# Cross attention's products with V issued in two halves, in a new order beside the scores; all heads written out; small changes at routing and at the expert tiles

## The reference, cut to what matters

```python
# cross attention, per head: 2048 queries, 1601 keys, 16 values each
scores = jnp.einsum('bhqd,bhkd->bhqk', q, k) / jnp.sqrt(jnp.float32(D_HEAD))
attn = jax.nn.softmax(scores, axis=-1)
out = jnp.einsum('bhqk,bhkd->bhqd', attn, v)
...
# experts
router_logits = jnp.einsum('bth,eh->bte', x, router_w)
topk_values, topk_indices = jax.lax.top_k(router_logits, TOP_K)
h1 = jax.nn.gelu(jnp.einsum('bth,efh->btef', x, w1) + b1, approximate=False)
expert_outputs = jnp.einsum('btef,ehf->bteh', h1, w2) + b2
```

## Time and profile before

| what | us |
|---|---|
| median of 3 runs (lowest to highest) | 2126.51 (2116.33 to 2149.73) |
| profiled execution, its own time | 2127.89 |
| span of the profile | 2126.1 |

### The profile page before, as it was taken

One profiled execution on the slowest core, in us unless ns is written; L12 is line 12 of the kernel. 1 busy time (PEld: TensorE's weight loads), 2 busy tenths in 40 slices (PEclk: granted clock), 3 DMA queues, 4 the chain that ended last, 5 costly groups with the idle time before them and its releaser, 6 DMA issues.

```text
span 2126.1 us, 35541 instructions
## 1 busy us (share of the span) xinstructions
PE 1815.0 (85%) x10422; PEld 930.1 (44%) x10422; DVE 1372.8 (65%) x2296; ACT 1190.3 (56%) x2400; POOL 360.3 (17%) x575
## 2 busy tenths in 40 slices
PE   6908899999899999987588888888888984999994
PEld 2504334333333333325243333333333244899993
DVE  6506899899898999815578888888888034011113
ACT  1200577777777777774047777777777541333333
POOL 6104022222222222110000000000000003233331
PEclk9956799999999999999579999999999565999997
DMA  6420001100001000002101001000002113566664
GB/s 232 164 101 16 3 25 36 35 28 25 27 26 34 28 35 27 3 1 78 61 32 65 26 21 38 21 27 32 20 31 68 40 42 119 151 204 192 192 193 136
DMA packets 72612, 140.12 MB, mean 66 GB/s; under 512 B 14140, under 2 KB 47309, under 8 KB 70237
## 3 DMA queue, kind: packets, MB, share of 16 engines
q1 hardware_dynamic: 64746, 127.84, 18.1%
q0 software_dynamic: 7712, 10.37, 2.3%
HBM read 109.07 MB, written 28.45 MB: 65 GB/s over the span
## 4 chain that ended last, share of the span: by engine, by line
PE 64%; DVE 17%; issue 6%; DMA 5%; ACT 4%; SPq 3%; POOL 1%; DVEq 0%; POOLq 0%; ACTq 0%
PE banks L910 19%; PE banks L900 16%; PE banks L862 12%; DVE CM L1317 6%; PE banks L1083 5%; PE banks L1093 5%; DMA W<-in_w1T_dram 2%; ACT XT L1149 2%; DVE wset L1324 2%; PE banks L816 2%; DVE skip L1324 2%; DVE CM L1320 2%; PE banks L820 1%; ACT late L1149 1%; PE banks L873 1%
## 5 line engine op out<-in xcount | busy, mean ns | idle before, releaser
L1149 ACT ACTIVATE XT<-banks 128x512 f32<-128x512 f32 x1240 | 671.9, 599 | 354.9 <-PE banks L900 249.6
L862 PE MATMUL banks<-oper 52*128 52x512 f32 (+1 forms) x2048 | 716.8, 446 | 107.5 <-DVE CM L1317 70.2
L900 PE MATMUL banks<-oper 54*128 54x512 f32 x1856 | 702.4, 465 | 37.4 <-ACT XT L1149 17.2
L1317 DVE TENSOR_REDUCE CM<-banks 128x1 f32<-128x804 f32 x512 | 486.4, 991 | 104.5 <-PE banks L862 104.5
L900 PEld LDWEIGHTS banks<-oper 54*128 54x128 f32 x1856 | 320.6, 191 | 428.1 <-ACT XT L1149 241.2
L862 PEld LDWEIGHTS banks<-oper 52*128 52x128 f32 x2048 | 344.1, 197 | 333.8 <-DVE CM L1317 202.9
L1149 ACT ACTIVATE late<-banks 128x512 f32<-128x512 f32 x616 | 337.5, 599 | 117.3 <-PE banks L900 101.3
L910 PE MATMUL banks<-XT,VS 128*32 128x512 f32 x2480 | 346.9, 632 | 2.7 <-ACT XT L1149 1.4
L1224 ACT ACTIVATE HID<-banks,b1E 128x128 f32<-128x128 f32 x312 | 89.1, 369 | 182.8 <-PE banks L1083 182.2
L1490 DVE TENSOR_TENSOR YB<-banks,b2E 128x256 f32<-128x256 f32 x39 | 16.6, 425 | 258.7 <-PE banks L1093 258.7
L910 PE MATMUL banks<-late,VS 128*32 128x512 f32 x1232 | 169.3, 622 | 0.8
(11 more groups left out here) (210 smaller groups left out, 1452.4 us busy)
## 6 DMA issues: line engine op xcount, KB each, us to landing
W<-in_w1T_dram SPq DMA_DIRECT2D x39, 1024.0 KB, 5.5
oper<-kD SPq DMA_DIRECT2D x32, 256.0 KB
W2R<-in_w2T_dram SPq DMA_DIRECT2D x8, 1024.0 KB, 8.5
oper<-kxD SPq DMA_DIRECT2D x32, 208.0 KB
b2E<-in_b_dram SPq DMA_DIRECT2D x39, 128.0 KB
qD<-parts SPq DMA_DIRECT2D x8, 512.0 KB, 2.7
kD<-parts SPq DMA_DIRECT2D x8, 512.0 KB, 2.7
oper<-kD SPq DMA_DIRECT2D x32, 128.0 KB
```

Source lines behind the costliest of these rows:

```text
L862: mm = pe.matmul(slot[:, n * QB:n * QB + ch], QO[64 * g:64 * g + M_ROWS, c2, col:col + P], KO[64 * g:64 * g + M_ROWS, c2, k0:k0 + ch], sta ...
L900: pe.matmul(bank, KO[64 * g:64 * g + S_ROWS, c, b * P:(b + 1) * P], QO[64 * g:64 * g + S_ROWS, c, q0:q0 + QB], start=True, stop=True).then ...
L1149: act.activation(PT[(c * plan.nu + u) % PRING], S[(c * plan.nu + u) % SBANKS], ACT.Exp).then_inc(A.exps, 1)
L1317: dve.tensor_reduce(CM[:, a, b:b + 1], slot.rearrange("p (n k) -> p n k", n=2)[:, :, 0:ch], AX.XY, ALU.max).then_inc(A.freed, 1)
```

## The change

- The head loop is gone: `head_steps` issues all 16 heads written out, on all engines, in both attentions.
- In cross attention each batch of V products is issued in two parts, queries 0 to 255 of each block and then 256 to 511 (`vparts` 2). The order within a slot is now a string of tokens: S0 to S3 the scores, m half a fill, V0 and V1 the parts of V. It is one string for slots with two fills and one for those with three. `order` gives the scores other query blocks so that neighbours fall into different groups. Self attention keeps its order.
- Norms: ACT saves the turned stream of group g-1 before it waits for the scales of group g, and PE does the router of group 2 before it turns group 3.
- Routing: DVE makes both halves of `OL`, POOL makes half of `OV` (the part with the tile numbers) in two instructions.
- Experts: SP issues the first weights of tile i ahead of the biases of tile i-2. The rows of tile i+2 are turned and saved where those of tile i+1 were, and ACT runs one small gelu before the first tile.
- `single` (one bank to a ring slot) is False in both plans and has no effect.

```diff
-    def __init__(self, nk, chunk, causal):
+    def __init__(self, nk, chunk, causal, single, vparts, sequences):
...
-        return (2, 0, 1, 3) if self.first((b + LEAD) % self.nb) % 2 == 0 else (0, 2, 3, 1)
+        if self.first((b + LEAD) % self.nb + 1) - self.first((b + LEAD) % self.nb) == 2:
+            kinds = (1, 1, 0, 0)
+        else:
+            kinds = (1, 0, 0, 1)
+        lead = self.first((b + LEAD) % self.nb) % 2
+        free = [[0, 1], [2, 3]]
+        return tuple(free[(kind + lead) % 2].pop(0) for kind in kinds)
...
-SELF = Plan(TT, QB, True)
-CROSS = Plan(NXP // P, XCH, False)
+SELF = Plan(TT, QB, True, False, 1, {2: "m S0 m S1 m S2 m V0 m S3"})
+CROSS = Plan(NXP // P, XCH, False, False, 2, {2: "S0 m S1 m V0 S2 m m S3 V1", 3: "m S0 m S1 m m S2 V0 m S3 m V1"})
...
-            body(0, 0, 0)
-            with engine.Fori(0, HEADS_LOOPED // RING) as it:
-                for c in range(RING):
-                    h = it * RING + (1 + c)
-                    body(h, (1 + c) % RING, it + (1 + c) // RING)
-            for h in range(HEADS_LOOPED + 1, H):
+            for h in range(H):
                 body(h, h % RING, h // RING)
...
-            for i in range(NTILES):
-                load_tile(i)
+            experts = []
+            for i in range(NTILES + WBUF - 1):
+                if i < NTILES:
+                    experts.append(expert_of(i))
+                    load_weights(i, experts[i])
+                if i >= WBUF - 1:
+                    load_biases(i - (WBUF - 1), experts[i - (WBUF - 1)])
...
-            pool.wait_ge(s_seat, 1)
-            for t in range(TT):
-                ins = pool.tensor_scalar(OL[:, TT + t, :], seatLo[:, :], lo[:, 1, t:t + 1], None, ALU.is_equal)
-            ins.then_inc(s_lot, 1)
+            pool.wait_ge(s_oh, 1)
+            for c in range(2):
+                half = slice(c * TT, (c + 1) * TT)
+                pool.tensor_tensor(OV[:, half, 1, :], OH[:, half, :], turns[:, :].unsqueeze(2).to_broadcast([P, TT, NBLK]),
+                                   ALU.mult).then_inc(s_lot, 1)
...
+                    w = QB // plan.vparts
+                    cols = slice(part * w, (part + 1) * w)
                     for n in range(4):
                         qb = plan.order(b)[n]
-                        mm = pe.matmul(OA[32 * qb:32 * qb + 32, :], VS[:, c, b, :], PT[(c * plan.nu + 4 * b + n) % PRING],
+                        mm = pe.matmul(OA[32 * qb:32 * qb + 32, cols], VS[:, c, b, :], PT[(c * plan.nu + 4 * b + n) % PRING][:, cols],
                                        start=(b == 0), stop=(b + 1 == nk), skip_group_check=True)
-                    mm.then_inc(A.pv, 1)
+                    if part + 1 == plan.vparts:
+                        mm.then_inc(A.pv, 1)
...
-                for g in range(NG - 2, NG):
-                    turn_stream(g)
-                    if call:
-                        router(g - 1)
+                turn_stream(NG - 2)
+                if call:
+                    router(NG - 3)
+                    router(NG - 2)
+                turn_stream(NG - 1)
...
             transpose_tile(0)
+            transpose_tile(1)
             for i in range(NTILES):
                 first_layer(i)
-                if i + 1 < NTILES:
-                    transpose_tile(i + 1)
+                if i + 2 < NTILES:
+                    transpose_tile(i + 2)
...
+            act.activation(odds[:, 3, :], odds[:, 0, :], ACT.Gelu)
             save_rows(0)
+            save_rows(1)
```

115 lines of the change are left out of this document (62 added, 53 removed).

## The result

| kernel | median us (lowest to highest, executions) | ratio to before, 95% interval |
|---|---|---|
| before | 2126.51 (2115.58 to 2149.73, 5) | 1 |
| changed | 2077.5 (2063.8 to 2131.93, 5) | 0.9724 (0.966 to 0.9788) |
| changed, six more executions | 2079.32 (2033.97 to 2109.41) | |

The change is a gain of 2 to 3%, about half of what was forecast (2010 us, range 1985 to 2066). One thing is needed to read the numbers: executions of the changed kernel differ by up to 98 us, by how long TensorE's clock stays at half, and the ratio is made from the quicker ones. The eleven lie almost on a line, from 2033.97 us at a mean granted clock of 0.922 to 2131.93 at 0.868. In time at half clock (twice the missing part of the clock, times the span) that is 317 against 562 us: each further microsecond at half clock costs 0.40. The median execution of the five has 432 us of it.

A forecast was written before the change was run, and what follows sets the result against it. No engine was saturated in cross attention, so a chain between PE, DVE and ACT was the bound. Self attention -19, cross attention -51, tail and transposes -34, norms -2, routing -5, experts -7: -118 from 2127.9, 2010 us, range 1985 to 2066.

The forecast's parts named there:

- heads 1 to 13, most of head 0 and half of head 14, 14.3 heads: Cross attention: heads counted as gaining 3.55 us each (35.4 for 38.95) from the split, -51 us; bounds -72 and -14.
- the clock falls in the tail again: Rival, end of cross attention: half clock returns because a 0.9 us gap remains; 2047 us in all, chance 0.20.
- bridge 0.77 us, and neither bridges 1.21: Cross attention: with PE away 0.77 us per half batch instead of 1.21, ACT and DVE keep working; 35.4 us a head.
- the two-part price 0.12 + 0.88: Cross attention's V batch: 0.12 us fixed plus a clock-scaled part; half a batch 0.12 + 0.44 = 0.56 at full clock.
- the 19 forecast: Self attention: writing out the head loop removes branch stalls, half-clock slots behind them and register work; -19 us, bounds 0 and 19.
- The waits come back: Rival, cross attention: waits reappear elsewhere in PE's fixed order, losing half the gain per head; 2035 or 2070 us, chance 0.15.
- fetched too slowly: Rival: the longer straight code cannot be fetched fast enough, so self attention's gain is lost; 2029 us, chance 0.06.
- nothing in cross attention: Rival: DVE sets the pace in cross attention anyway, so the change gains nothing there; 2061 us, chance 0.05.
- a half takes as long as a whole: Rival, cross attention: records, not columns, hold a half batch, costing 0.44 us more per half; 2193 us, chance 0.04.
- the forecast 2: Norms and router: half the last router run moves ahead of the last transposes, ACT saves earlier; -2 us, bounds -3.3 and 0.
- 4.1 of 5: Routing: DVE starts OL earlier since two products go to POOL, ending at 1788 for 1793.20; -5 us, bounds -6 and -2.
- the forecast 7: Experts: -2 us from rows saved before the table load and gelus, -5 from first weights issued a whole tile earlier.

## Why the prediction was wrong

**The step that failed** is the count of "heads 1 to 13, most of head 0 and half of head 14, 14.3 heads" at 3.55 us each. It took over from the kernel before that the clock is back at 1089, and priced every head at full clock. At half clock a head takes 60.5 us, 24.8 more. The first profile spent heads 0 to 2 and a part of head 3 so, the next one a part of head 0. The prediction had a rival for the clock, but only for the tail, and none of its five put it at the start. What the runs showed in its place: with V in halves the clock comes back 39 to 348 us behind the first score of head 0 (14.4 once), where it had been 11.7 in the kernel before. That the halves do this in the first heads is shown; by what means is open.

**What it cost.** The two columns are 112.5 us over the forecast in the first profile. The start holds 75.6 of it: 21.6 on the way to the first save, 2 x 24.8 for the next two heads and 4.4 for the third (40.11 for 35.73). In the tail the clock fell as well: the last two heads took 97.3 us, against 67.1 in the second profile, 30.2 more. The remaining 7 is the size of the gain per head and per slot. The fall in the tail is the rival "the clock falls in the tail again", given 0.20; it came true in one of the two profiles of the kernel. The argument against it, that self attention's last head kept its clock without fills, was weak: in seven of the fifteen other profiles 27 to 61 us at half clock begin in that head.

The median, 67 us over 2010, has no profile. By its mean clock it ran 432 us at half, 103 more than the second profile; at 0.40 each these make 41 us, and the two times are 39 apart.

**Right in number, wrong in cause.** The prediction had the waits go because PE is away for 0.77 us in place of 1.21: ACT and DVE "bridge 0.77 us, and neither bridges 1.21", so the split would give the whole 3.55 us a head. Of the 3.20 that came, the new order gives 1.98 with whole batches, where PE is away as long as before, and the halves add 1.22. Without the new order they give 1.16. A pair of slots, one with two fills and one with three, takes 5.88 us before, 5.45 with the new order alone and 5.31 with both. The prediction gave the order no gain of its own, so that its 5.32 for the pair came out is partly luck.

**Mis-sized a little.** 35.73 us a head for 35.4: 4 us in 13 heads. All of it is in shift and sum, which take 1.4 us a head (35.73 less 7 x 2.46 and 6 x 2.85) for the 1.0 to 1.1 assumed. The tail's slots at full clock: from the shift (1605.55) to the last save (1651.89) 46.3 us for 43.6. Of the 28 us by which the second profile missed 2010, 8.2 stand in the self heads (the last one ran partly at half clock and took 49.32 us), 12.8 on the way to the first cross save (half clock until 1107.0), and 6.6 in the cross heads, which is these two sizes.

**Right.** The half batch: 0.57 us to the next start, forecast 0.56; at half clock 1.01 (below), where the two-part price 0.12 + 0.88 says 1.00. DVE rows of 2.80 for three fills with 0.2 idle. PE's gap at the shift: 0.91, forecast 0.9. Self heads of 44.15 us but for the third (44.5) and the last, 16.8 us off their column in the first profile and 19.0 in that with the old order in the first two cross heads, for the 19 forecast. "The waits come back", "fetched too slowly", "nothing in cross attention" and "a half takes as long as a whole" were all wrong by the pitch of 35.73. The half batch at half clock, in PE's timeline of the changed kernel:

```profile
1129.55 1.08 PE L936 MATMUL banks<-XT,VS 128*32 128x256 f32 x8
1130.56 0.70 PE L885 MATMUL banks<-oper 52*128 52x402 f32 x1
```

**Behind cross attention** 17 was forecast for transposes, norms, routing and experts, and 13.8 came. Last save to router's end: 44.8 to 42.5, the same in both profiles, so 2.3 for the forecast 5. The transposes gave 2.7 of their 3: from the last save to the norm's first instruction on DVE it is 11.3 us before, at half clock, and 8.6 now, at full clock. The rows of the transposes of the head outputs, in the chain before and in that of now:

```profile
1728.49 1.99 PE banks L967 x8
...
1731.14 1.97 PE banks L967 x8
```

```profile
1745.83 0.67 PE banks L991 x4
...
1747.66 1.09 PE banks L991 x8
```

The norms and the router gave nothing for the forecast 2 (33.5 us from there to the router's end before, 33.9 now). The chain there in the changed kernel:

```profile
1764.19 3.69 PE banks L1001 x16
...
1773.41 6.62 PE banks L1021 x32
1780.04 1.81 PE banks L1013 x8
...
1782.53 3.59 PE banks L1021 x16
```

The router's last piece is 3.59 for 6.64, but the run of 6.62 ahead of it now delays the last transposes, as the bound of 0 for that term had it. Routing gained 4.1 of 5: the products on POOL end in time, but DVE's take 3.3 us each and no longer 2.38. Timeline of both engines, beside the earlier trace rows:

```profile
1797.46 4.81 POOL L804 TENSOR_TENSOR AT<-XT,turns 128x624 bf16<-128x624 bf16 x2 [22.23 <-DVE XT L1478]
```

```profile
1797.87 6.55 DVE L1483 TENSOR_TENSOR XT<-lo,seatLo 128x2048 bf16<-128x2048 f32 x2
```

From there to the end 7.3 for the forecast 7: PE's second tile starts without a wait and the waits for the first weights are gone, while ACT now waits for the first bias, which lands later, as the prediction said:

```profile
ACT HID L1251 <- DMA b1E<-in_b1T_dram: 159.6, 34, 6.4
```

These 159.6 us cost nothing: PE is busy 276.00 of 276 us in the expert tiles.

## What to carry to other kernels

Price a change to PE's work at both levels of the clock, and ask at which one each stage will start and how it gets back. When executions of one program differ, set their times against the mean granted clock before looking for another cause. The form that is quickest at full clock need not be the one that recovers it: here the slower form in two heads, and two products of no use in a gap of 0.9 us, were worth 2.2% and brought the scatter from 98 us to 12. And change one thing at a time before a gain is put down to it: here the order and the split each had a share.

## What the runs showed of the hardware

- A clock that does not come back although PE is busy: 194.63 of 195 us at 0.50; in the run with forced idle time 413.0 us at half, with a head of 79.1 us and three of 60.55. The Trainium skill ("TensorE: Matmul & The Clock Gate", Part 1) says that activity releases the throttle. In the first heads these traces agree for whole batches of V (back 5.6 to 15.9 us behind the first score). For halves (256 columns) being busy was not enough for up to 347.5 us, nor was it for whole batches in the tail (81.9 us in the kernel before). Why is open: shown is that the new order does not do it, and that forced idle time on PE does not help.
- The outcome differs between executions of one program: 256.0 and 102.4 us at half clock in two profiles of the changed kernel, and behind the gap of 0.9 us in the tail the clock fell in the one and stayed in the other.
- POOL slows beside DVE: of its two equal products the first takes 1.58 us and the second, all of it beside a large comparison on DVE, 3.27. In the kernel before, a spread on POOL takes 0.60 us while DVE is idle and up to 2.40 beside such a comparison. The Trainium skill ("GPSIMD Engine Reference", Specifications) says that POOL shares its SBUF interfaces with VectorE and that instructions of DVE with two SBUF inputs contend with it, which the comparisons have; the trace agrees.
- DVE's comparisons of 2.38 us take 3.32 and 3.31 in the changed kernel. That POOL is the cause is not shown: the one of 2.38 also ran beside POOL, and the last one ran its last 2.15 us after POOL had ended.
